# A two-layer decoder on one Trainium2 core: weight loads and region clearing moved from SyncE's own blocks into GpSimd's steps of the attention stages, and score tiles without filler rows

## What is computed

```python
x = x + rwkv_v4(norm(x))                                  # stage "rwkv"
x = x + cross_attention(norm(x), ctx_2048, band of 64)    # stage "xattn0": 8 heads, w_in, w_out, gated by ctx
x = x + ternary_mlp(norm(x))                              # stage "ffn0": weights quantised to -1, 0, 1 times a scale
x = x + causal_attention(norm(x))                         # stage "attn1": 16 heads
x = x + cross_attention_no_weights(norm(x), ctx_2048)     # stage "xattn1": 8 heads, no projections
x = x + top2_of_8_experts(norm(x))                        # stage "moe"
```

## Time and profile before

| | before |
|---|---|
| median of 3 runs | 2758.41 us (2756.8 to 2758.96) |
| the profiled execution's own time | 2778.94 us |
| its span | 2776.9 us |
| mean granted TensorE clock | 0.913 of full speed |
| busy: PE / PEld / DVE | 2217.8 / 1573.4 / 1868.5 us |
| busy: ACT / POOL | 1154.9 / 892.0 us |

### The profile page before, as it was taken

The page is one execution under the profiler, slowest core; times in us unless marked ns, Lnnn a source line. Parts: engine busy times, 40 slices in busy tenths (PEclk is TensorE's granted clock), DMA queues, the critical chain, the costliest instruction groups (busy, mean ns, idle before and its releaser), DMA issues. The chain is left out here.

```text
span 2776.9 us, 55137 instructions
## 1 busy us (share of the span) xinstructions
PE 2217.8 (80%) x19084; PEld 1573.4 (57%) x19084; DVE 1868.5 (67%) x5654; ACT 1154.9 (42%) x2616; POOL 892.0 (32%) x1488
## 2 busy tenths in 40 slices
PE   4787739999989982999959999388888888378796
PEld 3676626666666652999947777144444444245453
DVE  4999967787878767555526666478788786334245
ACT  1222215555555542222216666066666665132232
POOL 3565532222222214666630000232222221324422
PEclk9888859999999995999979999599999999589898
DMA  3000033333333310000030000533333331123434
GB/s 110 1 0 1 1 98 90 95 87 94 86 94 84 94 37 0 2 2 2 2 149 1 2 2 2 142 101 102 101 101 101 101 102 49 44 65 94 135 107 157
DMA packets 252306, 183.16 MB, mean 66 GB/s; under 512 B 29056, under 2 KB 246304, under 8 KB 251264
## 3 DMA queue, kind: packets, MB, share of 16 engines
q1 hardware_dynamic: 240416, 156.52, 20.4%
q0 software_dynamic: 7456, 18.92, 1.9%
q10 hardware_dynamic: 4160, 4.19, 0.5%
HBM read 94.47 MB, written 83.51 MB: 64 GB/s over the span
## 5 line engine op out<-in xcount | busy, mean ns | idle before, releaser
L764 ACT ACTIVATE xattn_pr<-ps 128x384 f32<-128x384 f32 (+1 forms) x1024 | 544.3, 542 | 459.6 <-PE ps L499 260.0
L483 PE MATMUL ps<-xattn_kp,xattn_qp 96*128 96x192 bf16 (+1 forms) x2048 | 375.0, 265 | 99.1 <-DVE xattn_mx L634 38.3
L496 PE MATMUL ps<-xattn_qp,xattn_kp 128*128 128x192 bf16 (+1 forms) x2048 | 412.0, 263 | 3.3 <-ACT xattn_pr L764 2.7
L634 DVE TENSOR_REDUCE xattn_mx<-ps 128x2 f32<-128x512 f32 x512 | 333.5, 678 | 119.7 <-PE ps L483 117.7
L514 PE MATMUL ps<-xattn_pr,xattn_vs 128*32 128x256 f32 (+1 forms) x4096 | 307.2, 372 | 35.1 <-ACT xattn_o L769 34.9
L630 DVE CUSTOM_DVE_ANT_0 xattn_masked<-ps,xattn_band 128x192 bf16<-128x192 f32 x1024 | 324.2, 354 | 13.2 <-issue 5.7
L496 PEld LDWEIGHTS ps<-xattn_qp,xattn_kp 128*128 128x128 bf16 x2048 | 178.7, 97 | 171.7 <-issue 91.1
L483 PEld LDWEIGHTS ps<-xattn_kp,xattn_qp 96*128 96x128 bf16 x2048 | 175.5, 99 | 176.7 <-DVE xattn_mx L630 60.6
L499 PE MATMUL ps<-xattn_band,xattn_ident 128*128 128x192 bf16 x1024 | 211.2, 247 | 0.0
L1002 PE MATMUL ps<-ffn_parts,gate_up_t 128*128 128x128 bf16 x3072 | 194.7, 220 | 2.1 <-DVE ffn_parts L1120 2.1
L1002 PEld LDWEIGHTS ps<-ffn_parts,gate_up_t 128*128 128x128 bf16 x3072 | 184.5, 99 | 16.4 <-DVE ffn_parts L1120 2.5
(11 more groups left out here) (304 smaller groups left out, 4548.6 us busy)
## 6 DMA issues: line engine op xcount, KB each, us to landing
xattn_rows<-xattn_parts SPq DMA_DIRECT2D x128, 192.0 KB, 2.1
xattn_qp<-xattn_rows SPq DMA_DIRECT2D x256, 96.0 KB, 2.8
xattn_kp<-xattn_rows SPq DMA_DIRECT2D x256, 96.0 KB, 3.1
xattn_rows<-xattn_parts SPq DMA_DIRECT2D x128, 128.0 KB, 2.1
moe_rows_in<-region_zero SPq DMA_DIRECT2D x6, 1677.0 KB, 7.4
moe_xb<-moe_rows_in SPq DMA_DIRECT2D x78, 129.0 KB
xattn_rows<-xattn_parts SPq DMA_DIRECT2D x128, 64.0 KB, 1.8
moe_row<-moe_rows_out SPq DMA_DIRECT2D x16, 512.0 KB, 8.4
```

The source lines that it names most:

```text
L483: mm = nc.tensor.matmul(ps[:, BANK_S + j % RING, mt * D:mt * D + width], qp[u][s][0:R_MAX, h, mt * P:(mt + 1) * P], kp[u][s][0:R_MAX, h, l ...
L496: mm = nc.tensor.matmul(out, kp[u][s][:, h, nt * P:(nt + 1) * P], qp[u][s][:, h, lo:lo + width], start=True, stop=not banded)
L634: ins = nc.vector.tensor_reduce(mx[s][:, h * NT:(h + 1) * NT], ps[:, BANK_S + j % RING, :].rearrange("p (m n) -> p m n", m=NT), AX.X, ALU.max)
L764: nc.scalar.activation(out, src, ACT.Exp, scale=HD ** -0.5).then_inc(exped, 1)
```

## The change

It does four things. (1) `begin_loads` is gone. POOL issues the loads, one per step, in steps p = 2, 3, ... of the wide attention, behind the reciprocal deviation. (2) `clear_regions` is gone. POOL clears `region_zero` in step 2 of the causal attention, and in steps 5, 9 and 13 changes its numbers and issues the two writes itself; it waits for the last of them at the stage's end. (3) `make_scores_t` contracts over partitions 0 to 98, so neither `qp` nor the rest of `kp` is filled beforehand: DVE's four memsets are gone, POOL fills a small tile `minus_one` (3 partitions x 2048) and copies it by four DMAs to partitions 96 to 98 of the `kp` tiles. (4) SP no longer waits for the presets; PE waits for the four small DMAs ahead of the first `make_scores_t`.

The diff, without new signatures, allocations and what only passes them on:

```diff
@@ begin_loads: the block that is gone @@
-    with core.nc.Block() as block:
-        @block.sync
-        def _(sp):
-            for to, of in loads:
-                sp.dma_start(to, of).then_inc(landed, 16)
@@ wide_attention @@
-    R_MAX = 96
+    R_MAX = ROWS * HD
+    R_ALL = R_MAX + PARTS
...
+    LATER_FROM = 2
+    later_loads, later_landed = later if later else ((), None)
...
+        minus_one = sb("minus_one", [PARTS, HW, D], BF16)
@@ SP, ahead of the first store @@
-                sp.wait_ge(preset, 1)
-                sp.wait_ge(k_preset, 1)
                 for p in range(2):
@@ PE, make_scores_t and the head of the stage @@
-                        mm = nc.tensor.matmul(out, kp[u][s][:, h, nt * P:(nt + 1) * P], qp[u][s][:, h, lo:lo + width],
+                        mm = nc.tensor.matmul(out, kp[u][s][0:R_ALL, h, nt * P:(nt + 1) * P], qp[u][s][0:R_ALL, h, lo:lo + width],
...
                     make_scores(1, 1, j)
+                pe.wait_ge(k_preset, 16 * 2 * S2)
@@ DVE, the head of the stage @@
-                for u in range(2):
-                    for s in range(S2):
-                        ins = nc.vector.memset(qp[u][s][:].rearrange("p h d -> p (h d)"), 0.0)
@@ POOL, its step and the head of the stage @@
                         fin.reciprocal_std(nc, g, p - 1)
+                    if 0 <= p - LATER_FROM < len(later_loads):
+                        to, of = later_loads[p - LATER_FROM]
+                        g.dma_start(to, of).then_inc(later_landed, 16)
+                nc.gpsimd.memset(minus_one[:].rearrange("p h d -> p (h d)"), -1.0).then_inc(minus_made, 1)
+                g.wait_ge(minus_made, 1)
                 for u in range(2):
                     for s in range(S2):
-                        ins = nc.gpsimd.memset(kp[u][s][:].rearrange("p h d -> p (h d)"), -1.0)
-                ins.then_inc(k_preset, 1)
+                        g.dma_start(kp[u][s][R_MAX:R_MAX + PARTS, :, :], minus_one[:]).then_inc(k_preset, 16)
                 left_overs(0, 0)
@@ clear_regions: its block becomes functions that POOL calls (SP's part is gone) @@
+    def zeros(self, nc, g):
+        nc.gpsimd.memset(self.zero[:].rearrange("p a d -> p (a d)"), 0.0).then_inc(self.made, 1)
...
+    def clear(self, nc, g, q):
+        wait(g, self.cleared, 16 * PARTS_R * q)
+        g.wait_ge(self.made, q + 1)
+        spare = self.core.c[:, C_SPARE + q * CLEAR:C_SPARE + (q + 1) * CLEAR]
+        nc.gpsimd.tensor_copy(self.zero[:, :, D:D + 1], spare.rearrange("p (a b) -> p a b", b=1)).then_inc(self.made, 1)
+        g.wait_ge(self.made, q + 2)
+        for h in range(PARTS_R):
+            to = self.x_in[h][q * P * CLEAR:(q + 1) * P * CLEAR, :].rearrange("(p a) d -> p a d", a=CLEAR)
+            g.dma_start(to, self.zero[:]).then_inc(self.cleared, 16)
@@ causal_attention, POOL @@
                         fin.reciprocal_std(nc, g, p - 1)
+                    if p == 2:
+                        regions.zeros(nc, g)
+                    if p >= 5 and (p - 5) % 4 == 0 and (p - 5) // 4 < regions.parts:
+                        regions.clear(nc, g, (p - 5) // 4)
...
                 fin.reciprocal_std(nc, g, PAIRS - 1)
+                regions.all_cleared(g)
```

More of the change, by code:

```diff
@@ L200, in reciprocal_std @@
         nc.gpsimd.tensor_tensor(self.core.stat[:, p, 1:2], self.rs[:], self.core.mhalf, ALU.pow).then_inc(self.rstd, 1)
-def begin_loads(core, name, loads):
-    landed = core.nc.alloc_semaphore(name=name)
-    with core.nc.Block() as block:
-        @block.sync
-        def _(sp):
-            for to, of in loads:
-                sp.dma_start(to, of).then_inc(landed, 16)
-    return landed, 16 * len(loads)
 def load_x(core, x_dram, const_dram, first, others, zeros, tiles):
@@ L287, in _, with wide_attention @@
                                         ALU.pow).then_inc(rstd, 1)
-def wide_attention(core, name, ctx_dram, w=None):
+def wide_attention(core, name, ctx_dram, w=None, later=None):
     nc, c, ps = core.nc, core.c, core.ps
@@ L1366 @@
 CLEAR = 13
-def clear_regions(core, ctx):
-    nc = core.nc
-    x_in = [nc.dram_tensor(f"moe_rows_in{h}", (ROWS, ROW), F32).ap() for h in range(PARTS_R)]
-    y_out = [nc.dram_tensor(f"moe_rows_out{h}", (2 * REGION + ROWS, D), F32).ap() for h in range(PARTS_R)]
-    zero = core.sb("region_zero", [P, CLEAR, ROW], ctx=ctx)
-    made, cleared = nc.alloc_semaphore(name="region_zero_made"), nc.alloc_semaphore(name="region_cleared")
-    parts = ROWS // (P * CLEAR)
-    with nc.Block() as block:
-        @block.gpsimd
-        def _(g):
-            nc.gpsimd.memset(zero[:].rearrange("p a d -> p (a d)"), 0.0).then_inc(made, 1)
-            g.wait_ge(made, 1)
-            for q in range(parts):
-                wait(g, cleared, 16 * PARTS_R * q)
-                spare = core.c[:, C_SPARE + q * CLEAR:C_SPARE + (q + 1) * CLEAR]
-                nc.gpsimd.tensor_copy(zero[:, :, D:D + 1], spare.rearrange("p (a b) -> p a b", b=1)).then_inc(made, 1)
-        @block.sync
-        def _(sp):
-            for q in range(parts):
-                sp.wait_ge(made, q + 2)
-                for h in range(PARTS_R):
-                    to = x_in[h][q * P * CLEAR:(q + 1) * P * CLEAR, :].rearrange("(p a) d -> p a d", a=CLEAR)
-                    sp.dma_start(to, zero[:]).then_inc(cleared, 16)
-    return (x_in, y_out), (cleared, 16 * PARTS_R * parts)
@@ new lines, with __init__, all_cleared @@
+class Regions:
+    def __init__(self, core, ctx):
+        nc = core.nc
+        self.core = core
+        self.x_in = [nc.dram_tensor(f"moe_rows_in{h}", (ROWS, ROW), F32).ap() for h in range(PARTS_R)]
+        self.y_out = [nc.dram_tensor(f"moe_rows_out{h}", (2 * REGION + ROWS, D), F32).ap() for h in range(PARTS_R)]
+        self.zero = core.sb("region_zero", [P, CLEAR, ROW], ctx=ctx)
+        self.made, self.cleared = core.sem("region_zero_made"), core.sem("region_cleared")
+        self.parts = ROWS // (P * CLEAR)
+    def zeros(self, nc, g):
[9 more added lines that the diff above has]
+            g.dma_start(to, self.zero[:]).then_inc(self.cleared, 16)
+    def all_cleared(self, g):
+        g.wait_ge(self.cleared, 16 * PARTS_R * self.parts)
@@ L2544, in decoder @@
             rows, loads = load_ternary(core, own, i['L0_ffn_w_gate_up'], i['L0_ffn_w_proj'])
-            landed = begin_loads(core, "ternary_landed", loads)
-            wide_attention(core, "xattn0", i['ctx_2048'], wide)
+            landed = nc.alloc_semaphore(name="ternary_landed")
+            wide_attention(core, "xattn0", i['ctx_2048'], wide, later=(loads, landed))
             core.end_stage()
-            gu, pj = ternary_weights(core, own, rows, landed)
+            gu, pj = ternary_weights(core, own, rows, (landed, 16 * len(loads)))
             gated_mlp(core, "ffn0", FF // 256, lambda j, kt, ft: gu[:, kt, (2 * j + ft) * P:(2 * j + ft + 1) * P],
@@ L2559, in decoder @@
         with ExitStack() as stage:
-            regions, cleared = clear_regions(core, stage)
-            causal_attention(core, "attn1", attn, b_q, b_k, b_v, b_o)
-            nc.sync.wait_ge(*cleared)
+            regions = Regions(core, stage)
+            causal_attention(core, "attn1", attn, b_q, b_k, b_v, b_o, regions)
         core.end_stage()
@@ L2566, in decoder @@
             experts, loads = load_experts(core, own, *(i[f'L1_ffn_W{n}'] for n in 'rgud'))
-            landed = begin_loads(core, "experts_landed", loads)
-            wide_attention(core, "xattn1", i['ctx_2048'])
+            landed = nc.alloc_semaphore(name="experts_landed")
+            wide_attention(core, "xattn1", i['ctx_2048'], later=(loads, landed))
             core.end_stage()
-            routed_experts(core, "moe", experts, regions, out, landed, rwkv)
+            routed_experts(core, "moe", experts, regions, out, (landed, 16 * len(loads)), rwkv)
 def kernel(**inputs):
```

10 lines of the change are left out of this document (5 added, 5 removed).

## The result

The changed kernel takes 3359.36 us in the median (3349.55 to 3367.93, 4 runs) against 2758.05 us for the one before in the same session: a ratio of 1.2179 (95% interval 1.2140 to 1.2219). I had forecast 2712.5 us and given 0.03 to anything slower. The profiled execution took 3367.93 us, with a span of 3366.0 us and a mean granted clock of 0.757, where before it was 0.913.

The account below looks back on a forecast made before the run. PE was taken as close to full in steady attention, so gains lay between stages. 3.6 + 1.9 (xattn0), 24.1 - 2.1 (attn1) and 12.6 + 5.8 (xattn1) made 45.9 us, taking 2758.4 to 2712.5 us; range 2706 to 2727.

Parts of the forecast that it names:

- part 6: Weight loads of the contraction over 99 rows: the number of rows does not show in their duration, so nothing counted.
- The change takes nothing from PE's steady work: Steady parts of the attention stages, PE close to full: they cannot give anything back and can only lose.
- slow loading: Rival: weight loads of 99 rows fall back to 190 ns, 190 us lost less 46 won, 2903 us; chance 0.03.
- Part 1: Heads of xattn0 and xattn1: without the two load blocks they start 3.6 and 12.6 us earlier, 16.2 us won.
- part 2: Between ffn0 and attn1: without the clearing block attn1 starts at about 1418.1 in place of 1442.13, 24.1 us won.
- part 4: Clearing inside attn1: POOL's fill holds DVE and stalls one normalise, 2.1 us lost.
- Part 3: Heads of the wide attentions: POOL's first subtraction comes sooner, 1.9 us won in xattn0 and 5.8 in xattn1.
- that rival: DVE holds POOL's four small issues at the wide attentions' heads: 13.6 us less won, 2726 us; chance 0.08.
- The rule that I cited: Trainium skill: a GpSimd-issued DMA stalls while VectorE uses both its ports; at the heads, an estimated 10 us more.
- Part 5: Thirteen loads issued by POOL inside the wide attentions: 1.1 us per gate-up, 1.7 per expert load, hidden, nothing counted.
- the rival of dear issues: POOL's issues of expert loads in the wide attentions are dear: 13 us lost of the 45.9, 2725.5 us; chance 0.13.

Follow-up runs that it names:

- x3: Kernel before, with only make_scores_t contracting over partitions 0 to 98 in place of 0 to 127; 2759.12 us, ratio 1.0003.
- after: The changed kernel itself, make_scores over 48 partitions and make_scores_t over 51; 3359.36 us, ratio 1.2179 to the kernel before.
- x1: Changed kernel with the tiles, fills and SP waits of the kernel before (96 and 128 partitions contracted); 2722.48 us, ratio 0.9870 to the kernel before.
- x9: As x1, but make_scores over 65 partitions and make_scores_t over 68; 2848.10 us, ratio 1.0314 to the kernel before.
- x2: Kernel before with only its tiles changed to 48 and 51 partitions, load and clearing blocks kept; 3399.16 us, ratio 1.2321.

## Why the prediction was wrong

- **The step that failed is part 6**, "Contraction over 99 rows ... nothing". It failed twice. The number was misread (48 and 51, not 96 and 99), and the price was taken from the duration of a weight load, which hardly changed (102 ns for 97). Neither the spacing of matmuls nor the clock shows in that duration. At the size that I had read, the step holds (x3, ratio 1.0003).
- **Its worth.** The difference between after's profiled span and x1's is 3366.0 - 2724.5 = 641.5 us. The scores' stretches hold 451.7 (xattn0) and 184.7 (xattn1) of it, 636.4 together. In xattn0 some 140 us are changes of class by themselves, some 74 us the clock with few partitions, and some 238 us their meeting. In xattn1 the tiles add only 0.4 changes per head, an estimated 0.42 x 512 x 0.10 = 22 us at full clock, and the rest of the 184.7 us goes with the lower clock, as in x9, which adds no change there and loses 115.7. Why the clock falls stays open.
- **"The change takes nothing from PE's steady work ... It can only cost them something"** was the right sentence, but I looked for that cost only in POOL's and SP's steps, and gave the tiles a single rival, slow loading, at 0.03. That rival had the right place and the wrong mechanism: the loads are hardly slower; at a change of class they start later, and the clock is lost besides.
- **Part 1 and part 2** (16.2 and 24.1 us) and the stall of part 4 (2.1 us) were right: their sum of 38.2 us came out at 35.5 (x1). Singly the blocks gave 3.6 and 12.1 us, attn1 starts 1.2 us behind ffn0 in place of 25.2, and the stall held one `normalise` by 2.15 - 0.41 = 1.7 us. The 39.8 us between x2 and after, both of which have the short heads, fit, but their scores' stretches differ by 14.7 us.
- **Part 3**: first subtractions at 5.7 and 4.2 us for 5.6 and 4.3 forecast, and the four small issues 2.18 us for 2.3. DVE did not hold them, so that rival is out. The rule that I cited for it is not refuted: beside the issues DVE had only casts and memsets of 0.11 to 0.91 us and the end of one `normalise`, and no run shows which of these take both of its ports. I had taken DVE's 3.79 us as given; it shrank to 2.22 with the shorter hold, but ACT's part came no earlier than forecast.
- **Part 5**: an expert load's issue took 0.97 us, less than the 1.7 I took (and far less than 7.7). No wait of PE for it appears; the rival of dear issues is out.
